# Normalisations moved from their own blocks into the first expert mixture, a new drive block, and scans moved into the recall

## The reference

```python
def _L0_ffn_ref(x, ...):            # first mixture, 16 experts, top 2
    y = x + moe
    return (y - mu) / jnp.sqrt(var + EPS) * gamma + beta

def _L1_attn_ref(embeddings, E, Dx, Dy):   # embeddings = layernorm(h)
    def step(carry, v_prev):
        x_update = relu(v_prev @ Dx.T)                       # "drive"
        x_t = 0.97 * x_state + x_update
        x_t = x_t / maximum(sum(abs(x_t)), 1e-12)            # "levels"
        a_star = einsum('bdn,bn->bd', rho, x_t)              # "recall"
        y_t = relu(_ln(a_star) @ Dy.T) * relu(x_t)
        v_star = _ln(y_t @ E.T)                              # "answer"
        rho_t = 0.97 * rho + _ln(v_prev)[:, :, None] * x_t[:, None, :]
        ...

h = h + _L0_ffn_ref(_layernorm(h), ...)
h = h + _L1_attn_ref(_layernorm(h), ...)
h = h + _L1_ffn_ref(_layernorm(h), ...)      # second mixture, 8 experts
```

## Time and profile before

| what | value |
|---|---|
| time, median of 3 | 2327.01 us (2314.51 to 2331.49) |
| time of the profiled execution | 2307.62 us |
| its span | 2305.8 us |
| busy: PE, PEld, DVE, ACT, POOL | 1901.9, 837.1, 1279.9, 1081.3, 247.3 us |
| granted TensorE clock, mean | 0.894 of 2.4 GHz |

### The profile page before, as it was taken

One profiled execution on the slowest core, in us unless ns is written; L12 is line 12 of the kernel. 1 busy time (PEld: TensorE's weight loads), 2 busy tenths in 40 slices (PEclk: granted clock), 3 DMA queues, 4 the chain that ended last, 5 costly groups with the idle time before them and its releaser, 6 DMA issues. The chain is left out here.

```text
span 2305.8 us, 42367 instructions
## 1 busy us (share of the span) xinstructions
PE 1901.9 (82%) x15788; PEld 837.1 (36%) x15788; DVE 1279.9 (56%) x3321; ACT 1081.3 (47%) x2031; POOL 247.3 (11%) x252
## 2 busy tenths in 40 slices
PE   6948989898989898994699999138459995899999
PEld 2311222222222222221344444013249973444444
DVE  2449877787878688811444443668764442233331
ACT  1312776676767576772345554025123321455454
POOL 2111000000000000001000000223001332000000
PEclk9956999999999899996799999569669985899999
DMA  5441111111112120001475634000000000324221
GB/s 218 151 88 19 26 41 26 36 27 37 30 32 40 31 37 23 23 16 36 90 144 109 125 79 77 1 2 0 1 4 2 1 1 21 78 46 86 45 58 39
DMA packets 85769, 112.29 MB, mean 49 GB/s; under 512 B 29786, under 2 KB 70836, under 8 KB 83532
## 3 DMA queue, kind: packets, MB, share of 16 engines
q1 hardware_dynamic: 80984, 100.53, 20.6%
q0 software_dynamic: 3104, 8.72, 1.0%
q10 hardware_dynamic: 1492, 0.46, 0.1%
HBM read 90.89 MB, written 18.79 MB: 48 GB/s over the span
## 5 line engine op out<-in xcount | busy, mean ns | idle before, releaser
L780 ACT ACTIVATE b_prob<-b_p_s 128x512 f32<-128x512 f32 x1104 | 570.7, 603 | 327.3 <-PE b_p_s L936 310.7
L801 DVE TENSOR_REDUCE b_m<-b_p_m 128x1 f32<-128x1024 f32 x512 | 603.5, 1218 | 149.2 <-PE b_p_s L936 118.0
L888 PE MATMUL b_p_m<-b_k,b_q 48*64 48x512 bf16 x2048 | 377.5, 423 | 66.7 <-DMA b_k<-qk_scr 22.4
L936 PE MATMUL b_p_s<-b_q,b_k 51*64 51x512 bf16 x2048 | 359.8, 404 | 9.4 <-ACT b_prob L780 8.7
L964 PE MATMUL b_p_o<-b_prob,v_all 128*9 128x512 f32 x2304 | 311.8, 625 | 1.0
L888 PEld LDWEIGHTS b_p_m<-b_k,b_q 48*64 48x64 bf16 x2048 | 95.2, 109 | 451.8 <-DVE b_m L801 261.4
L1276 ACT ACTIVATE d_hidden<-d_p_z 128x704 f32<-128x704 f32 x192 | 135.0, 755 | 130.9 <-PE d_p_z L1193 130.9
L1276 ACT ACTIVATE n_hidden<-n_p_z 128x704 f32<-128x704 f32 x192 | 135.0, 755 | 127.3 <-PE n_p_z L1193 127.3
L1387 DVE TENSOR_TENSOR d_xg<-d_xd,d_c_wide 128x352 f32<-128x352 f32 x192 | 96.2, 521 | 103.9 <-PE d_p_z L1193 80.0
L1193 PE MATMUL d_p_z<-d_xg,d_w 64*128 64x352 f32 x768 | 142.2, 485 | 12.6 <-DVE d_xg L1387 12.6
L1193 PE MATMUL n_p_z<-n_xg,n_w 64*128 64x352 f32 x768 | 142.6, 486 | 8.6 <-DVE n_xg L1387 8.6
(11 more groups left out here) (303 smaller groups left out, 2264.5 us busy)
## 6 DMA issues: line engine op xcount, KB each, us to landing
d_c_wide<-d_c_scr SPq DMA_DIRECT2D x48, 704.0 KB, 14.4
n_c_wide<-n_c_scr SPq DMA_DIRECT2D x48, 352.0 KB, 7.7
xt<-in_x SPq DMA_DIRECT2D x16, 1024.0 KB, 8.9
sum_scr<-b_sums POOLq DMA_DIRECT2D x32, 256.0 KB, 2.6
b_q<-qk_scr SPq DMA_DIRECT2D x96, 66.0 KB
qk_scr<-a_qk_part SPq DMA_DIRECT2D x24, 256.0 KB, 2.8
b_k<-qk_scr SPq DMA_DIRECT2D x16, 198.0 KB
b_k<-qk_scr SPq DMA_DIRECT2D x16, 132.0 KB
```

What stands on the lines that cost most here:

```text
L780: nc.scalar.activation(prob[:, U % PR_RING, 0:w], p_s[:, U % S_RING, 0:w], ACT.Exp, scale=float(D) ** -0.5).then_inc(exp_done, 1)
L801: nc.vector.tensor_reduce(m3[:, x, 0:1], p_m[:, s, :, :].rearrange("p k n -> p (k n)"), axis=AX.X, op=ALU.max).then_inc(rows_free, 1)
L888: last = nc.tensor.matmul(out[e:e + 64, k, :], q_st[s][r, i, t * P + e:t * P + e + 64], k_st[s][r, i, k * WIDE:k * WIDE + WIDE], start=Tru ...
L936: last = nc.tensor.matmul(out[e:e + 64, :], k_st[s][r, q, jt * P + e:jt * P + e + 64], q_st[s][r, q, a * WIDE:a * WIDE + WIDE], start=True ...
```

## The change

The affine block, the level block and the state block are gone as blocks. Each sample's three layer norms (of the mixture's sum, of `hid` for the drive, of that again for the recall) are now made by `feed_*` helpers inside the first mixture: statistics on VectorE (`feed_measure` nine `bn_stats`, `feed_gather` nine `bn_aggr`), everything else on GpSimd. `feed_enter` has five wide operations of 128 x 576, `feed_drive` and `feed_recall` two each. Samples 6 and 7 are only partly through when the mixture ends; the rest is done in the drive block.

The drive block is new: `v` is written twice side by side by ScalarE (`double`), turned as 128 x 128 (in pieces of 4, 4 and 1 tiles through one PSUM bank), and multiplied on the two row halves of the array, both feature halves at once. The relu writes `u_all` itself. VectorE adds the two halves (`join`), and three products a sample add into one PSUM sum over all samples. `levels` is the old chain with one more scaling by 0.97, its sums read from PSUM. The rates go to DRAM. The recall block loads them back, spread over the partitions by DMA (528 KB a sample, three buffers), and runs the 16 scans itself, three ahead of the first mask and then two a sample, at t = 0 and t = 8. Powers of 0.97 moved into `tri`, the state copy and `eT`. `free_sems` runs once, behind the recall, instead of behind the affine block.

```diff
+            if feed:
+                feed_load(g, sp, feed)
...
-            for b in range(B):
+            def rstd_of(b):
                 pool.wait_ge(moments, NT * (b + 1))
                 nc.gpsimd.tensor_tensor(rs[:, 1, :], mv[:, :, 1], g.eps[:, :], ALU.add).then_inc(rstd, 1)
                 pool.wait_ge(rstd, 2 * b + 1)
                 nc.gpsimd.tensor_tensor(rs[:, 0, :], rs[:, 1, :], g.minus_half[:, :], ALU.pow).then_inc(rstd, 1)
+
+            for b in range(2):
+                rstd_of(b)
+            for it in range(B):
+                if feed and it >= 2:
+                    feed_drive(g, pool, feed, it - 2)
+                if it + 2 < B:
+                    rstd_of(it + 2)
+                if feed and it >= 1:
+                    feed_enter(g, pool, feed, it - 1)
+                if feed and it >= 2:
+                    feed_recall(g, pool, feed, it - 2)
...
+                    if feed and it >= 1 and gi == 8:
+                        dve.wait_ge(misc_free, out_use(it - 1, 1) + 1)
+                        feed_measure(g, dve, feed, 0, it - 1)
+                    if feed and it >= 1 and gi == 9:
+                        feed_gather(g, dve, feed, 0, it - 1)
+                    if feed and it >= 2 and gi == 3:
+                        feed_measure(g, dve, feed, 1, it - 2)
+                        feed_gather(g, dve, feed, 1, it - 2)
+                    if feed and it >= 2 and gi == 10:
+                        feed_measure(g, dve, feed, 2, it - 2)
+                    if feed and it >= 2 and gi == 11:
+                        feed_gather(g, dve, feed, 2, it - 2)
             for r in range(2):
                 add_out(B - 1, r)
-
...
-def affine_block(g, pre, xn_all, gamma_arg, beta_arg):
...
-def drive_block(g, u_all, vn_all, level):
...
+def feed_measure(g, dve, feed, k, b):
+
+    nc, rows = g.nc, g.hid if k == 1 else feed["sums"]
+    if k:
+        dve.wait_ge(feed["step"][k - 1], FEED_STEPS[k - 1] * (b + 1))
+    dve.wait_ge(feed["moments"][k], NT * b)
+    for t in range(NT):
+        nc.vector.bn_stats(feed["st"][:, k, t, :], rows[:, b, t, :]).then_inc(feed["stats"][k], 1)
+
...
+def feed_gather(g, dve, feed, k, b):
+    nc = g.nc
+    dve.wait_ge(feed["stats"][k], NT * (b + 1))
+    if b:
+        dve.wait_ge(feed["step"][k], FEED_STEPS[k] * b)
+    for t in range(NT):
+        nc.vector.bn_aggr(feed["mv"][:, k, t, 0:2], feed["st"][:, k, t, :]).then_inc(feed["moments"][k], 1)
...
+def feed_rstd(g, pool, feed, k, b, n):
+    nc, mv, step = g.nc, feed["mv"][:, k, :, :], feed["step"][k]
+    pool.wait_ge(feed["moments"][k], NT * (b + 1))
+    pool.wait_ge(step, n)
+    nc.gpsimd.tensor_tensor(mv[:, :, 3], mv[:, :, 1], g.eps[:, :], ALU.add).then_inc(step, 1)
+    pool.wait_ge(step, n + 1)
+    nc.gpsimd.tensor_tensor(mv[:, :, 2], mv[:, :, 3], g.minus_half[:, :], ALU.pow).then_inc(step, 1)
...
+def feed_normalise(g, pool, feed, k, n, out, rows):
+    nc, mv, step = g.nc, feed["mv"][:, k, :, :], feed["step"][k]
+    pool.wait_ge(step, n)
+    nc.gpsimd.tensor_tensor(out, rows, mv[:, :, 0:1].to_broadcast([P, NT, D]), ALU.subtract).then_inc(step, 1)
+    pool.wait_ge(step, n + 1)
+    nc.gpsimd.tensor_tensor(out, out, mv[:, :, 2:3].to_broadcast([P, NT, D]), ALU.mult).then_inc(step, 1)
...
+def feed_enter(g, pool, feed, b):
+
+    nc, step, n, x = g.nc, feed["step"][0], FEED_STEPS[0] * b, feed["sums"][:, b, :, :]
...
+    feed_rstd(g, pool, feed, 0, b, n)
+    feed_normalise(g, pool, feed, 0, n + 2, x, x)
+    pool.wait_ge(step, n + 4)
+    pool.wait_ge(feed["w_in"], 48)
+    nc.gpsimd.tensor_tensor(x, x, wide(feed["gamma"]), ALU.mult).then_inc(step, 1)
+    pool.wait_ge(step, n + 5)
+    nc.gpsimd.tensor_tensor(x, x, wide(feed["beta"]), ALU.add).then_inc(step, 1)
+    pool.wait_ge(step, n + 6)
+    nc.gpsimd.tensor_tensor(g.hid[:, b, :, :], g.hid[:, b, :, :], x, ALU.add).then_inc(step, 1)
...
+def feed_drive(g, pool, feed, b):
+
+    n = FEED_STEPS[1] * b
+    pool.wait_ge(feed["step"][0], FEED_STEPS[0] * (b + 1))
+    feed_rstd(g, pool, feed, 1, b, n)
+    feed_normalise(g, pool, feed, 1, n + 2, feed["sums"][:, b, :, :], g.hid[:, b, :, :])
...
+def feed_recall(g, pool, feed, b):
+
+    nc, step, n, mv = g.nc, feed["step"][2], FEED_STEPS[2] * b, feed["mv"][:, 2, :, :]
+    pool.wait_ge(feed["step"][1], FEED_STEPS[1] * (b + 1))
+    feed_rstd(g, pool, feed, 2, b, n)
+    pool.wait_ge(step, n + 2)
+    pool.wait_ge(feed["w_in"], 48)
+    nc.gpsimd.tensor_tensor(mv[:, :, 2], mv[:, :, 2], feed["grow"][:, :], ALU.mult).then_inc(step, 1)
+    feed_normalise(g, pool, feed, 2, n + 3, feed["vn"][:, b, :, :], feed["sums"][:, b, :, :])
...
+            sp.wait_ge(level_step, 9)
+            sp.dma_start(rate_scr[:, :], rate[:, :]).then_inc(rate_sent, 16)
+            sp.wait_ge(rate_sent, 16)
...
+            feed_drive(g, pool, feed, B - 2)
+            feed_enter(g, pool, feed, B - 1)
+            feed_recall(g, pool, feed, B - 2)
+            feed_drive(g, pool, feed, B - 1)
+            feed_recall(g, pool, feed, B - 1)
...
+            def turn(b, k):
...
+                pe.wait_ge(vT_ready, 3 * b + k)
+                pe.wait_ge(w_ready, 2)
+                lo, hi = PIECES[k]
+                for t in range(lo, hi):
+                    last = nc.tensor.transpose(p_turn[:, (t - lo) * P:(t - lo) * P + P], twice[:, b % 2, t, :, :].rearrange("p q d -> p (q d)"), g.eye[:])
+                last.then_inc(turned, 1)
...
+            def drive(b, a):
...
+                if n >= 2:
+                    pe.wait_ge(relu_done, n - 1)
                 for f in range(2):
-                    for a in range(NC):
-
-                        last = nc.tensor.matmul(p_sum[0:B, a, 0:CH], col[:, :], u[:, f, a * CH:a * CH + CH],
-                                                start=(f == 0), stop=(f == 1), skip_group_check=True)
+                    r = slice(f * D, f * D + D)
+                    last = nc.tensor.matmul(p_u[:, n % 2, f, 0:CH], dxT[r, :], vT[r, b % 2, a * CH:a * CH + CH], start=True, stop=True)
+                last.then_inc(driven, 1)
...
+            def add_up(b):
+                pe.wait_ge(joined, b + 1)
+                for a in range(NC):
+                    last = nc.tensor.matmul(p_sum[0:B, a, 0:CH], column[:, b, :], both[:, b % 2, a * CH:a * CH + CH],
+                                            start=(b == 0), stop=(b == B - 1), skip_group_check=True)
                 last.then_inc(summed, 1)
...
+            for k in range(3):
+                turn(0, k)
+            for b in range(B):
+                for k in range(3):
+                    drive(b, k)
+                    if b + 1 < B:
+                        turn(b + 1, k)
+                if b:
+                    add_up(b - 1)
+            add_up(B - 1)
...
+            def double(b):
+                act.wait_ge(feed["step"][1], FEED_STEPS[1] * (b + 1))
+                if b >= 2:
+                    act.wait_ge(turned, 3 * (b - 1))
+                nc.scalar.copy(twice[:, b % 2, :, :, :], v[:, b, :, :].unsqueeze(2).to_broadcast([P, NT, 2, D])).then_inc(doubled, 1)
...
+            for n in range(NC * B):
+                b, a = divmod(n, NC)
+                if a == 0 and 1 <= b < B - 1:
+                    double(b + 1)
+                act.wait_ge(driven, n + 1)
+                nc.scalar.activation(u_all[:, b, :, a * CH:a * CH + CH], p_u[:, n % 2, :, 0:CH], ACT.Relu).then_inc(relu_done, 1)
...
+                nc.vector.tensor_copy(vT[:, b % 2, lo * P:hi * P], p_turn[:, 0:(hi - lo) * P]).then_inc(vT_ready, 1)
...
+            def join(b):
...
+                nc.vector.tensor_tensor(both[:, b % 2, :], u_all[:, b, 0, :], u_all[:, b, 1, :], ALU.add).then_inc(joined, 1)
...
+                nc.vector.tensor_scalar(rate[:, :], small[:, :], DECAY, None, ALU.mult).then_inc(level_step, 1)
...
+            nc.vector.tensor_copy(dxT[:, :], p_turn[:, 0:P]).then_inc(w_ready, 2)
+            for k in range(3):
+                keep(0, k)
+            feed_measure(g, dve, feed, 1, B - 2)
+            feed_gather(g, dve, feed, 1, B - 2)
+            feed_measure(g, dve, feed, 0, B - 1)
+            feed_gather(g, dve, feed, 0, B - 1)
+            for b in range(B):
+                if b + 1 < B:
+                    for k in range(3):
+                        keep(b + 1, k)
+                if b == 1:
+                    feed_measure(g, dve, feed, 2, B - 2)
+                    feed_gather(g, dve, feed, 2, B - 2)
+                if b == 2:
+                    feed_measure(g, dve, feed, 1, B - 1)
+                    feed_gather(g, dve, feed, 1, B - 1)
+                join(b)
+            levels()
+            feed_measure(g, dve, feed, 2, B - 1)
+            feed_gather(g, dve, feed, 2, B - 1)
...
+            def spread_rate(b):
+                if b >= RATES:
+                    sp.wait_ge(scanned, 2 * (b - RATES) + 2)
```

(20 more changed lines are left out.)

328 lines of the change are left out of this document (80 added, 248 removed).

## The result

The changed kernel takes **2164.07 us** (median of four runs, 2159.68 to 2169.63), the kernel before 2324.91 (four runs): a ratio of **0.9327, 95% interval 0.9286 to 0.9367**. Forecast were 2181, 2156 to 2215. The profiled execution has a span of 2157.6 us; forecast was 2160.

What follows compares the result with a forecast made beforehand. TensorE bounds the mixture and the recall's middle; in 253.8 us between no engine is full. -167.5 + 4.7 + 8.2 + 6 + 3 = -145.6 gives span 2160, time 2181 us, range 2156 to 2215.

Steps and rivals of the forecast that it cites:

- The move: Mixture's end to recall's start: blocks of 253.8 us replaced by a new drive block, recall beginning at 1536.5 not 1704.0, -167.5 us.
- the 6 to 6.5 that were to show it: Drive block: predicted sign that the sums come every 6 to 6.5 us; every 11 would mean clock 0.50.
- The mixture: First mixture: late xg pairs from mutual VectorE-GpSimd waiting cost half a us in each of six samples, +3 us.
- The start of the recall: Recall's start: rates load 4 us, then three scans, put mask 0 at 10.9 us instead of 6.1, +4.7 us.
- Scans inside: Recall: thirteen scans mostly hidden in VectorE's idle time, losing time at changes of sample, +8.2 us, bounds 5 and 30.
- The semaphores: Behind the recall: clearing 86 semaphores at 0.07 us each where only a handover stood, +6 us (3 to 7).
- The span: Whole profiled execution: terms sum to -145.6 us, taking the span from 2305.8 to 2160 us.
- From the span to the time: Whole kernel: the earlier profile's 0.8% distance under its median carried over, turning span 2160 into time 2181 us.
- The mixture's: Rival, first mixture: mutual waiting costs much more, half of the 71 us bound, 35, so 2213 us; chance 0.12.
- the clock's: Rival, drive block: TensorE stays at 1.2 GHz, 11 us a sample instead of 6.05, +34, 2215 us; chance 0.08.
- GpSimd's: Rival, first mixture: GpSimd's chain becomes the bound and the kernel is slower, 2330 us and more; chance 0.02.
- the scans were hidden: Answers a rival, recall: scans not hidden, VectorE becomes the bound, +22, 2203 us; chance 0.12.

## Why the prediction was right, and where it was off

**The move** (-167.5; -171.2). Right, and shown by undoing it: 101 to 103 us of it come from the normalisations alone. The drive block came 3.2 us sooner to its levels (60.3 instead of 63.5 from the first load). The first drive product came 9.1 us in instead of 10.3, and the sums every 5.80 to 5.87 us, laid out as 6.05, which is some 1.5 us over seven samples (and less than the 6 to 6.5 that were to show it). The levels (14.6; 14.9) and the tail with its handover (7.2; 7.7) were right, and cutting the tail's chain showed it to be this chain.

**The mixture** (+3; +0.2). The mutual waiting was argued from one direction in the earlier trace rows and is real in both: 2.07 us more for a pair of `xg`. The step that failed is where it falls. I put the last wide operations of `feed_enter` on the pair right behind the ranking, with 1.7 us of room; they fell on the pair ahead of it, which TensorE wanted 3.3 us after it was done. With every wide operation doubled they did reach the pair behind the ranking; it came 1.2 us late, and of the room 0.45 us was left. So the lateness was mis-sized too (2 to 2.6 us forecast). Gamma and beta take 1.40 us each on GpSimd, where I took 1.17; that lies off the path.

This agrees with the Trainium skill (SBUF — State Buffer, section "SBUF: two separate sides"), by which the shared ports are an exclusive lock for a whole instruction; of GpSimd's powers that does not hold here (see the end). What decides the price in these runs is the idle time around the collision.

**The start of the recall** (+4.7; +4.9). The sum was right (rates landed 4.15 us behind the start of the first load, taken as 4; three scans 6.86), but its reading was incomplete: taking one scan away gained 0.1 us, since TensorE's start at 8.3 us, behind the other loads, is a second bound that close below the first.

**Scans inside** (+8.2; +5.9). By change of sample 2.3, 1.8, 0.2 and three times 1.3 were laid out; 1.9, 1.2, 0 and three times 0.7 came. The mechanism was right (two scans close together, and a GpSimd add behind them). The late changes are the term that was mis-sized: GpSimd's wide operation and the first scan do overlap in the way described, as the changed kernel's timeline shows, but I let the second scan wait for the whole add (1.4 us). The add begins to run while VectorE is at its statistics and mask, and the second scan is held off by 0.46 us only (2.81 instead of 2.35).

```profile
1651.90 1.17 POOL L1767 TENSOR_TENSOR k_v_sb<-k_v_sb,k_v_mv 128x576 f32<-128x576 f32 x1
...
1652.11 3.17 DVE L1987 TENSOR_TENSOR_SCAN m_x_all<-m_x_all,k_rate 128x1056 f32<-128x1056 f32 x1
...
1653.14 3.34 POOL L1769 TENSOR_TENSOR hid<-hid,k_v_sb 128x576 f32<-128x576 f32 x1
```

The scan holds off the add (3.34 us instead of 1.40), and GpSimd's wide operation the scan (3.17 instead of 2.35).

**The semaphores** (+6; +6.3). Right, confirmed by leaving the clearing out.

**The span** (-145.6; -148.2). 2.6 us apart is closer than the terms deserve: the stretches that the change touches came to -153.9, 8.3 us more than forecast, and the stretches ahead of them and behind, forecast at nothing, gave 5.8 back. That they met is luck.

**From the span to the time** (2160 to 2181; 2157.6 to 2164). Here are 14.5 of the 17 us by which the forecast was high. I carried over the 19 us between the profiled run of before and its median as though they were part of the kernel. They are not. Attention, the same in all, ended anywhere from 1077.8 to 1100.2 in the 14 profiles, at a mean of 1088. The profile of before had one of the fastest. When the changed kernel was profiled again, its first DMA came at 1100.23, and this time the profiled run lay 8.8 us above its median, not below.

What differs between them is TensorE's granted clock. Windows from the start to the mixture's first DMA, in the run without the clearing and in the changed kernel's second profile (the kernel before has 0.92 too):

```profile
0.00:1077.82 1077.82, 912.13 (x10010) 272.14 (x10010) 728.22 (x879) 621.58 (x1209) 87.73 (x106) 0.92 0.20 49
```

```profile
0.00:1100.23 1100.23, 938.54 (x10010) 275.31 (x10010) 728.02 (x879) 621.39 (x1209) 87.75 (x106) 0.89 0.19 48
```

VectorE and ScalarE are busy for the same time to 0.3 us, TensorE for 26 us more, at a clock of 0.89 instead of 0.92. The executions without a trace have their mean clock on record, and it goes the same way: of the last eleven of the kernel before the shortest (2301.57) had 0.897, the longest (2325.24) 0.883. That attention is where they differ is likely, not shown; the distance of the profile of before to the mean would cover 9 of the 17 to 19 us. Why the clock differs between runs of the same program stays open.

**The rivals.** The mixture's, the clock's and GpSimd's did not come; the scans were hidden to 5.9 of 30 us. The clock's was nearer than its chance said: 1.2 GHz for 20.5 us. What that costs is some 2 us by the two profiles in which it was 13.6, and going from 10.2 us down to 3.4 gained nothing more, as the filled gaps show, since VectorE was the bound there.

## What to carry over

Count a block between two dense stages as its whole length if its engines idle in the neighbour. Moving it there costs what falls on the neighbour's rooms, and rooms are to be read pair by pair, not as a mean. At the seams that remain, look for the next bound behind the one that you remove: a scan taken away from the start bought 0.1 us, and a clock brought back 7 us sooner bought nothing, each because a second wait ended close below. A room of some us in one block is also the first thing that doubling the work there uses up: ask of each wait how far away the next one is. And compare a profiled run with its median only after reading where an untouched stage ended in it, and at which clock.

## What was unexpected

- An untouched stage of 1.08 ms ends within a spread of 22 us in 14 profiles on at least four chips, and four of them on one and the same chip already span it (1077.8 to 1100.1). The granted clock of the stage goes with it, 0.92 to 0.89. From there on two profiles of the changed kernel differ by 3.4 us.
- Filling TensorE's gaps with 32 transposes cut the stretch at a granted clock of 0.50 to 3.4 us, from 10.2 in the same kernel without them; issuing two loads early had cut it from 20.5 to 10.2. The same beginning of the block had 20.5 us in four profiles and 13.6 in two.
- One RECIPROCAL over 8 partitions x 1056 takes 6.74 us of the levels' 14.6, in a chain where nothing else runs; a scan of the same length takes 2.35.
- A power on GpSimd (128x9, 1.80 us) did not hold off VectorE: the pair of `xg` that began at 1198.62, beside one, took 1.12 us as elsewhere. In the changed kernel 22 `xg` products overlap such a power, in all 14 profiles 312, and none took more than 0.55 us. A wide GpSimd operation of 1.17 to 1.40 us made one take up to 1.72.
